# Rests of up to 64 rows of two experts share a page, 72 tiles in place of 79

## What is computed

```python
scores = softmax(xt @ Wg.T)                      # 2048 tokens, 16 experts in 4 groups
gidx   = top_k(max of scores in each group, 2)   # two groups of a token
topi   = top_k(scores in those groups, 4)        # four experts of a token
weights = scores[topi]
h = silu(einsum('td,eid->eti', xt, W1)) * einsum('td,eid->eti', xt, W3)   # 176 wide
expert_out = einsum('eti,edi->etd', h, W2)
y = einsum('etd,te->td', expert_out, combine)    # combine holds the weights
z = silu(xt @ Ws1.T) * (xt @ Ws3.T) @ Ws2.T      # shared experts
x = layernorm(x + y + z)
```

## Time and profile before

| | us |
|---|---|
| median of 3 runs | 1193.8 |
| lowest and highest | 1188.15, 1194.08 |
| the profiled execution | 1193.7 |
| its span, first to last instruction | 1191.9 |
| TensorE busy (matmuls) | 1087.6 (91%) |
| VectorE busy | 496.3 (42%) |
| ScalarE busy | 504.1 (42%) |
| POOL busy | 439.9 (37%) |
| mean granted TensorE clock | 0.964 |

### The profile page before, as it was taken

The page is one execution under the profiler, slowest core; times in us unless marked ns, Lnnn a source line. Parts: engine busy times, 40 slices in busy tenths (PEclk is TensorE's granted clock), DMA queues, the critical chain, the costliest instruction groups (busy, mean ns, idle before and its releaser), DMA issues. The chain is left out here.

```text
span 1191.9 us, 29025 instructions
## 1 busy us (share of the span) xinstructions
PE 1087.6 (91%) x10260; PEld 838.5 (70%) x10261; DVE 496.3 (42%) x1340; ACT 504.1 (42%) x1306; POOL 439.9 (37%) x563
## 2 busy tenths in 40 slices
PE   8889989988898679999988999998789999999998
PEld 4466666655455347777756777786579899899997
DVE  2366665545571113333325666767443800000323
ACT  2444544444432123333334666575344333333333
POOL 2022131311248852777654666332524000200434
PEclk9999999999999669999999999999789999999999
DMA  6199478021283334565536111000157555555673
GB/s 202 45 311 362 161 237 268 21 81 55 118 258 118 129 113 126 154 191 150 144 120 284 37 37 53 22 19 3 56 194 237 187 175 177 174 175 174 194 240 107
DMA packets 119339, 176.09 MB, mean 148 GB/s; under 512 B 17440, under 2 KB 96912, under 8 KB 117776
## 3 DMA queue, kind: packets, MB, share of 16 engines
q1 hardware_dynamic: 94448, 135.55, 34.9%
q0 software_dynamic: 9696, 26.75, 6.9%
q10 hardware_dynamic: 15088, 12.28, 3.1%
HBM read 105.07 MB, written 68.16 MB: 145 GB/s over the span
## 5 line engine op out<-in xcount | busy, mean ns | idle before, releaser
L3149 PE MATMUL bank<-w,m_HT 128*128 x624 | 141.0, 379 | 0.0
L2984 ACT ACTIVATE m_HT<-bank,m_b 128x128 f32<-128x128 f32 x312 | 88.9, 370 | 90.2 <-PE bank L3135 74.2
L3149 PEld LDWEIGHTS bank<-w,m_HT 128*128 128x128 f32 x624 | 115.7, 190 | 14.1
L1820 PE MATMUL bank<-m_W,m_XGT 128*128 x316 | 114.0, 485 | 9.0 <-ACT m_XGT L1677 6.8
L1434 POOL DMA_INDIRECT GA<-ys,r_pos x64 | 64.7, 1010 | 62.9 <-DVE m_US L1764 43.0
L1677 ACT ACTIVATE m_XGT<-bank 128x256 f32<-128x256 f32 x79 | 30.3, 384 | 129.2 <-DVE m_US L1764 80.1
L1756 DVE TENSOR_TENSOR m_H<-bank,m_SG 128x176 f32<-128x176 f32 x79 | 26.9, 341 | 135.7 <-ACT m_SG L1681 96.9
L2948 POOL DMA_INDIRECT m_GA<-ys,r_pos x32 | 31.6, 986 | 133.6 <-SPq L2904 124.9
L3135 PE MATMUL bank<-m_XGT,m_w1a 128*128 128x128 f32 x640 | 77.3, 279 | 2.6 <-issue 1.8
L1820 PEld LDWEIGHTS bank<-m_W,m_XGT 128*128 128x128 f32 x316 | 56.6, 199 | 30.2 <-issue 14.3
L3135 PEld LDWEIGHTS bank<-m_XGT,m_w1a 128*128 128x128 f32 x640 | 75.0, 195 | 3.5 <-issue 2.3
(11 more groups left out here) (475 smaller groups left out, 2301.3 us busy)
## 6 DMA issues: line engine op xcount, KB each, us to landing
m_w1a<-in_m_w SPq DMA_DIRECT2D x20, 1024.0 KB
m_w<-in_m_w SPq DMA_DIRECT2D x19, 1024.0 KB
xs<-zeros SPq DMA_DIRECT2D x1, 10112.0 KB, 34.2
ys<-zeros SPq DMA_DIRECT2D x1, 10112.0 KB, 34.6
ys<-m_US ACTq DMA_DIRECT2D x79, 128.0 KB
m_GS<-xs SPq DMA_DIRECT2D x72, 128.0 KB
w<-in_m_w SPq DMA_DIRECT2D x8, 1024.0 KB, 11.9
xs<-zeros SPq DMA_DIRECT2D x1, 6400.0 KB, 23.7
```

The source lines that it names most:

```text
L1820: last = nc.tensor.matmul(BU[b % 2][:, 0:IW], XGT[:, b % 2, m * P:(m + 1) * P], W13[:, m, bass.ds(e, 1), :], start=m == 0, stop=m == KC - 1)
L2984: last = nc.scalar.activation(HT[:, b % 2, at, :], BU[i][:, c * P:(c + 1) * P], ACT.Gelu, bias=b1[:, b % WB, at:at + 1])
L3149: last = nc.tensor.matmul(BY[b % 2][:, 0:DIM], HT[:, b % 2, c, :], w2[:, bass.ds(e, 1), c, :], start=c == 0, stop=c == CH - 1)
```

## The change

An expert's rest, the rows behind its last full page, no longer takes a page of its own if it has at most 64 rows. Two such rests share a page: one in its lower 64 rows, one in its upper 64. The padding is counted in half pages: `NS0 = ceil(((8192 + 16*63) // 64) / 2) = 72`. Shared pages are the last eight (`MIXED0 = 8`), so tiles 64 to 71 (`PURE = 64`) are computed as if they had two experts, whether they have or not. The table gets a fourth row, `second`, the expert of the upper half.

- Routing: `halves` in place of the last part of `on_dve`, some more steps in `order_on_dve` and `ready_on_dve`.
- TensorE in tiles 64 to 71: each matmul of the up and down product is two, with 64 stationary columns each, into rows 0 to 63 and 64 to 127 of the bank; the second takes its weights from `UPS` and `DOWNS`.
- VectorE copies the second expert's weights there (`keep_up` five steps ahead, `keep_down` three), three sets in turn, in the memory of `Z`.
- Straight code for the last 12 (TensorE), 16 (VectorE) and 8 (ScalarE) tiles; the moments at tile 44, the root after token tile 7, the apply within step 62.
- `EARLY` is 11: token tiles 11 to 15 are gathered in rounds 0 to 4 of `layer1`.

```diff
+HALF = P // 2
+MIXED0 = E0 // 2
...
+    def halves(self, do, dve, v, c, count, slots, total, thresholds, rank_bank):
+        e, k, pad = self.e, self.k, self.e // 2
+        each = lambda ap: ap.unsqueeze(1).broadcast_to([P, TILES, e])
+        nt, single = self.nt[:, 0, pad:], self.nt[:, 1, pad:]
+        do(dve, v.tensor_scalar(self.low[:], count, float(HALF), None, ALU.subtract))
+        do(dve, v.tensor_tensor(c, self.low[:].unsqueeze(2).broadcast_to([P, e, TILES]),
+                                thresholds.unsqueeze(1).broadcast_to([P, e, TILES]), ALU.is_gt))
+        do(dve, v.tensor_reduce(nt, c, AX, ALU.add))
+        do(dve, v.tensor_scalar(self.most[:], nt, float(P), None, ALU.mult))
+        do(dve, v.tensor_tensor(single, count, self.most[:], ALU.is_gt))
+        src, dst, d = self.nt, self.ends, 1
+        while d < e:
+            do(dve, v.tensor_tensor(dst[:, :, pad:], src[:, :, pad:], src[:, :, pad - d:pad + e - d], ALU.add))
+            src, dst, d = dst, (self.ends2 if dst is self.ends else self.ends), 2 * d
+        ends, first, self.singles, self.single = src[:, 0, pad:], dst[:, 0, pad:], src[:, 1, pad:], single
+        self.end_tile, self.first_row = ends, first
+        do(dve, v.tensor_tensor(slots, slots, rank_bank[:, 0:TILES * e].rearrange("p (t e) -> p t e", e=e), ALU.add))
+        do(dve, v.tensor_tensor(first, ends, nt, ALU.subtract))
+        do(dve, v.tensor_scalar(first, first, float(P), 0.0, ALU.mult, ALU.add))
+        do(dve, v.tensor_scalar(self.from_page[:], ends[:, e - 1:e], float(self.slot_tiles - e // 2), None, ALU.max))
+        do(dve, v.tensor_scalar(self.move[:], ends, self.from_page[:, 0:1], -2.0, ALU.subtract, ALU.mult))
+        do(dve, v.tensor_tensor(self.move[:], self.move[:], self.singles, ALU.add))
+        do(dve, v.tensor_tensor(self.move[:], self.move[:], single, ALU.subtract))
+        do(dve, v.tensor_tensor(self.masked[:], slots, each(self.most[:]), ALU.is_ge))
+        do(dve, v.scalar_tensor_tensor(out=self.masked[:], in0=each(self.move[:]), scalar=float(HALF), in1=self.masked[:],
+                                       op0=ALU.mult, op1=ALU.mult))
+        do(dve, v.tensor_tensor(self.slot[:], slots, each(first), ALU.add))
+        do(dve, v.tensor_tensor(self.slot[:], self.slot[:], self.masked[:], ALU.add))
...
-EARLY = 12
+EARLY = 11
...
-                    if t == 9:
+                    if t == 7:
                         fx.l1.root_on_pool(nc, pool, fx.neghalf, own)
...
-                tile_pipeline(act, step, NT)
+                tile_pipeline(act, step, NT, peel=8)
...
+                    if ahead is None:
+                        return
+                    if 0 <= j + 5 - PURE < MIXED0:
+                        keep_up(j + 5 - PURE)
+                    if 0 <= j + 3 - PURE < MIXED0:
+                        keep_down(j + 3 - PURE)
+                    if j == 62:
+                        fx.l1.apply_on_dve(nc, dve, fx.X)
+                def keep_up(n):
+                    e = experts[n] = dve.value_load(r.second[0:1, PURE + n:PURE + n + 1], min_val=0, max_val=E0 - 1)
+                    if n == 0:
+                        dve.wait_ge(z_added, 2 * TILES)
+                    r.steps(dve, nc.vector.tensor_copy(UPS[:, n % SETS].unsqueeze(2), W13[:, :, bass.ds(e, 1), :]))
+                    up_step[n] = r.steps.k
+                def keep_down(n):
+                    e = experts.pop(n)
+                    nc.vector.tensor_copy(DOWNS[:, n % SETS, 0:1, :], W2A[:, bass.ds(e, 1), :])
+                    r.steps(dve, nc.vector.tensor_copy(DOWNS[:, n % SETS, 1:2, :], W2B[:, bass.ds(e, 1), :]))
+                    down_step[n] = r.steps.k
...
-                tile_pipeline(dve, step, NT, ((56, lambda: fx.l1.moments_on_dve(nc, dve, fx.X, r.steps)),
-                                              (68, lambda: fx.l1.apply_on_dve(nc, dve, fx.X))))
+                tile_pipeline(dve, step, NT, ((44, lambda: fx.l1.moments_on_dve(nc, dve, fx.X, r.steps)),), peel=16)
...
+                    if mixed is not None:
+                        pe.wait_ge(r.steps.sem, up_step[mixed])
...
+                        nc.tensor.matmul(BU[b % 2][0:HALF, 0:IW], XGT[:, b % 2, m * P:m * P + HALF],
+                                         W13[:, m, bass.ds(e, 1), :], start=m == 0, stop=m == KC - 1)
+                        last = nc.tensor.matmul(BU[b % 2][HALF:P, 0:IW], XGT[:, b % 2, m * P + HALF:(m + 1) * P],
+                                                UPS[:, mixed % SETS, m, :], start=m == 0, stop=m == KC - 1)
...
+                    pe.wait_ge(r.steps.sem, down_step[k])
+                    for c, w2 in enumerate((W2A, W2B)):
+                        nc.tensor.matmul(BY[b % 2][0:HALF, 0:DIM], HT[:, b % 2, c, 0:HALF], w2[:, bass.ds(e, 1), :],
+                                         start=c == 0, stop=c == 1)
+                        last = nc.tensor.matmul(BY[b % 2][HALF:P, 0:DIM], HT[:, b % 2, c, HALF:P],
+                                                DOWNS[:, k % SETS, c, :], start=c == 0, stop=c == 1)
...
-                tile_pipeline(pe, step, NT)
+                tile_pipeline(pe, step, NT, peel=12)
...
-        fx.NS0 = (TOKENS * TOP0 + E0 * (P - 1)) // P
+        fx.NS0 = -(-((TOKENS * TOP0 + E0 * (HALF - 1)) // HALF) // 2)
```

More of the change, by code:

```diff
@@ L1002, in __init__ @@
         self.gmax, self.grank = sb("gmax", [P, TILES, max(groups, 1)]), sb("grank", [P, TILES, max(groups, 1)])
-        self.nt, self.ends, self.ends2 = (sb(n, [P, e // 2 + e]) for n in ("nt", "ends", "ends2"))
+        rows = [2] if groups else []
+        self.nt, self.ends, self.ends2 = (sb(n, [P, *rows, e // 2 + e]) for n in ("nt", "ends", "ends2"))
+        self.fields = 4 if groups else 3
+        if groups:
+            self.most, self.move, self.own2 = (sb(n, [P, e]) for n in ("most", "move", "own2"))
+            self.from_page, self.at_half = sb("from_page", [P, 1]), sb("at_half", [P, 1])
+            self.upto_half, self.of_half = sb("upto_half", [P, 2, e]), sb("of_half", [P, 2])
         self.hot = sb("hot", [P, k, TILES, e])
@@ L1116, in on_dve @@
         count, slots = self.upto[:, TILES - 1, :], dst[:, pad:]
+        if self.groups:
+            do(dve, v.tensor_tensor(slots, self.upto, total, ALU.subtract))
         if not self.groups:
@@ L1213, in order_on_pe @@
         pe.wait_ge(self.steps.sem, self.table_step)
-        nc.tensor.matmul(table_bank[:, 0:3 * self.slot_tiles], ones[:], self.vals[:].rearrange("p i n -> p (i n)"),
+        nc.tensor.matmul(table_bank[:, 0:self.fields * self.slot_tiles], ones[:], self.vals[:].rearrange("p i n -> p (i n)"),
                          start=True, stop=True).then_inc(self.counted, 1)
@@ L1408, with tile_pipeline @@
 PEEL = 7
-def tile_pipeline(engine, step, n, visits=(), done=0):
-    for at, visit in (*visits, (n - PEEL, None)):
+def tile_pipeline(engine, step, n, visits=(), done=0, peel=PEEL):
+    for at, visit in (*visits, (n - peel, None)):
         with engine.Fori(done // 4, at // 4) as i:
@@ L1419, in tile_pipeline @@
         done = at
-    for j in range(n - PEEL, n):
+    for j in range(n - peel, n):
         step(j, j % 4, n - 1 - j)
```

83 lines of the change are left out of this document (58 added, 25 removed).

## The result

The changed kernel takes 1177.47 us (median, 1173.65 to 1178.36) where the kernel before took 1192.85 (four executions, the three of the table ahead of the prediction among them): 15.4 us less by the medians, 13.2 by the ratio, which is 0.9889 with a 95% interval of 0.9856 to 0.9922 (9.3 to 17.2 us). The record doesn't name the chip of this first comparison. The forecast was 1188.4, with a range of 1181 to 1197. Sign right, size wrong by 10.9 us. In three further groups of runs, on two chips, the ratio was 0.9905 (0.9873 to 0.9938), 0.9938 (0.9916 to 0.9960) and 0.9895 (0.9874 to 0.9917): 11.3, 7.4 and 12.5 us. Both that spread and the median have to be explained.

The account below looks back on a forecast made before the run. The prediction took the first expert stage, in its full stretch, to be bound by TensorE alone. Its terms, -17.5 + 2.9 + 5.3 + 1.5 + 2.5 = -5.3 us, took 1193.7 to 1188.4 us, range 1181 to 1197.

Parts of the forecast that it names:

- Part 1: First expert stage: seven tiles fewer on TensorE, at 2.497 us each, give -17.5 us.
- Part 2: Routing: more vector instructions ahead of the positions, which POOL's first scatter waits for, cost +2.9 us.
- the scatter, the end of it and the start of the full stretch move by as much: POOL's scatter: its start, its end and TensorE's full stretch all come 2.9 us later.
- Part 3: Last eight tiles: halved products run two at a time, +0.66 us each, +5.3 in all; weight copies +1.5.
- rival (a): Shared tiles: the halves run serially, eight tiles cost 19.7 us in place of 5.3, total 1202.8; chance 0.08.
- a change of shape: Shared tiles on TensorE: switching array shape costs some 0.1 us, four times a tile, so 0.4.
- the half-pass tail: Shared tiles on TensorE: half a pass left at the end of each product, 0.15 + 0.11 = 0.26 us.
- Rival (b): Weight copies: VectorE, blocked by POOL, lags and TensorE waits, +8 us in place of 1.5, total 1194.9; chance 0.17.
- Part 4: Moved steps: moments, root and apply cost 0; EARLY 11 adds a gather round in layer 1, +2.5 us.
- 0, for the root is a short POOL instruction: Layernorm: moving the root up two token tiles costs nothing, with only POOL's own next fetch behind it.
- They leave the full stretch, not the scatter's, since the scatter's length is unchanged: First expert stage: the seven tiles leave the steady stretch; eight or so stay in the time of the 64 scatters.
- The forecast's own sign of being wrong: First expert stage: the prediction is wrong if, among other signs, the full stretch doesn't start 2.9 us later.

Follow-up runs that it names:

- before_warm: The kernel before with six more TensorE products of 256 columns in each of the first twelve tile steps: 1204.91 us.
- after_warm: The changed kernel with six more TensorE products of 256 columns in each of the first twelve tile steps: 1196.53 us.
- after: The changed kernel in the first comparison and its trace, against the kernel before: 1177.47 us, ratio 0.9889.
- early12: The changed kernel with EARLY 12 in place of 11: 1193.05 us, ratio 0.9959 to the kernel before.
- tiles72: The kernel before with 72 tiles in place of 79, apply at tile 60, eight tiles peeled, EARLY still 12: 1216.78 us, ratio 1.0154.
- groups 2, 3 and 4: Sets of runs beside the kernel before, each on one chip: group 1 on chip 4, 2 and 4 on chip 13, 3 and 5 on chip 9.
- before: The kernel before, unchanged, in the first comparison and its traces: 1192.85 us in the first comparison.
- delay: The kernel before with ten more vector instructions ahead of the positions, three of 256 columns and seven of 16: 1198.19 us, ratio 1.0011.
- after_third: The changed kernel, unchanged, a third time, beside the kernel before in group 3: 1190.38 us, ratio 0.9938.
- whole_products: The changed kernel with whole products in the last eight tiles and no weight copies, second experts left out: 1189.75 us, ratio 0.9928 to the kernel before.
- after_again: The changed kernel, unchanged, in a second session, group 2: 1178.59 us, ratio 0.9905 to the kernel before.
- after_fourth: The changed kernel, unchanged, once more in group 4: 1177.90 us, ratio 0.9895 to the kernel before.
- halves_in_turn: The changed kernel with all lower-half products written ahead of the upper-half ones in place of alternating: 1177.74 us.
- after_gap: The changed kernel with two more products of 256 columns ahead of the up product in each of the first eight steps: 1182.10 us.
- moved72: The kernel before with 72 whole pages and the change's moved steps, EARLY 11 and peel counts, no halves or copies: 1175.93 us, ratio 0.9895.
- before_fourth: The kernel before, unchanged, in group 5: 1140.48 us.
- delay_again: The kernel before with ten more vector instructions ahead of the positions, again, in group 5: 1142.88 us, ratio 1.0002.
- before_warm8: The kernel before with three more TensorE products of 256 columns in each of the first eight tile steps: 1203.55 us.
- before_third: The kernel before, unchanged, a third trace, beside the changed kernel in group 3: 1196.94 us.

## Why the prediction was wrong

**Part 1, the price of seven tiles: right (where they leave from was not, see below).** 2.50 us a tile in both kernels' full stretch (2.50 to 2.52 from y10 to y59 in all traces but before_warm and after_warm); y10 to y59 takes 122.5 us in after (442.93 to 565.40), and 49 x 2.497 is 122.4.

**Part 2, the way to the positions: right at its start, too dear at its end.** The first scatter is at 344.97 us on the mean of nine traces with the halves, at 341.79 on that of nine without: +3.2 for the forecast 2.9, single traces 2 us to either side. But the last scatter moves by 1.9 between the same two sets (437.55 and 435.68). The step "the scatter, the end of it and the start of the full stretch move by as much" failed by 1.0 us: the 64 scatters of the later start took a little less time.

**Part 3, shared tiles: mechanism right, the size too large by 2.6 us.** The halves run two at a time, rival (a) is out. The period is 3.09 us, +0.59 for the forecast 0.66: the rows' turning, the up product, the product's turning and the down product each take 0.15 us longer (0.37 against 0.22, 1.33 against 1.19, 0.37 against 0.21, 1.01 against 0.87), so a change of shape and the half-pass tail are one cost and not two. That is 0.6 us of the 2.6. The copies cost one wait of 0.42 us, not 1.5, which is 1.1 us of the 2.6. Rival (b) never came, though a wide copy did double beside POOL. The rest, 0.9, is probably that the last tiles drain, 1.2 to 1.5 us apart, where the forecast charged a full 0.66 to each of the eight. The page "TensorEngine Tiling (Array Packing)" of the Trainium skill, section "Key Properties", says both that tiles operate independently and that a switch of the tiling mode drains TensorE. The trace agrees with the first (starts 0.01 us apart); of the second it shows 0.15 us for each switch, and not the drain itself.

**Part 4: right.** The fifth gather round is 28.0 us in place of 25.6, +2.4 for 2.5. early12 shows the other side: with the gather kept in the stage, layer 1 starts 7.2 us late, for 2.4 given back. tiles72 shows what I had costed at nothing: without the earlier root TensorE waits 15.4 us. "0, for the root is a short POOL instruction" holds for the change as made.

With the measured terms the sum is -17.5 + 1.9 + 4.2 + 2.4 = -9.0 us in place of -5.3. Three things agree with it. The group in which both kernels show the same stretch gave -7.4 (-10.1 to -4.8). The other groups' intervals by the ratio hold 9.0 or miss it by under 1 us (9.3 to 17.2, 7.4 to 15.1 and 9.9 to 15.0 us less), so the executions alone barely tell these gains from 9.0; that there is a surplus rests on the traces. And a line fitted through all executions of a group, time against mean granted clock with an offset for the changed kernel, puts that offset at -8.9 (standard error 1.1), -7.7 (0.7) and -9.6 (1.1) in groups 2, 3 and 4. The fit takes the clock as given, which it may not be: among the traces without added products, the stretches with more waiting are those with the lower clock.

**The step that failed** is the one under Part 1: "They leave the full stretch, not the scatter's, since the scatter's length is unchanged". The tiles inside the scatter's stretch were taken as a constant of the kernel ("eight or so"). The forecast's own sign of being wrong came: the full stretch did not start 2.9 us later, y10 came 4.7 earlier. The tiles in the stretch are no constant: from 390 to 436 us the traces show 6 result copies (before, three times, and also delay, tiles72, after_third, early12 and whole_products), 8 (after, after_again, after_fourth, halves_in_turn, after_gap), 9 (moved72), 18 (before_fourth) and 19 (delay_again). Of the 6.4 us between 9.0 and 15.4, two tiles more are 5; the last scatter came 1.1 us later in this pair of traces where 1.9 is the mean. The terms that were too dear (1.0 in part 2, 2.6 in part 3) are the other 3.6 of the miss. A single trace of before could not show that the stretch varies, but it did show that in it no visible work explains the 7 to 10 us between two copies, and I didn't ask what does.

**What is settled and what isn't.** Shown: in the first pair of traces the surplus over 9.0 us lies in that stretch; it can be missing with the change in place (after_third, whole_products), and the short distance can be there without the halves (moved72). The idle time there is of a kind that can vanish for the unchanged kernel (before_fourth). Not shown: that the change brings the two tiles. Outside the first comparison the form goes with the chip: 11.8 to 14.4 us of distance in all seven traces of groups 1 and 3 without added products for TensorE, 3.9 to 6.1 in the four of groups 2 and 4. The unchanged kernel was not traced on chip 13, where only its times are known, 1179 to 1197 us, wide enough to hold both forms. The one pair that differs is the first, from one trace each, and whether the two ran on one chip isn't on record. That a higher clock doesn't bring the tiles is likely from before_warm8, but its added products took time of their own. Open too: why engines wait there for nothing that the profile names. Since groups 3 and 5 bear the same chip number and differ by 56 us, it need not be the chip; what else differed isn't on record. What the change is worth where the kernel before takes 1142 us was not tried: there the fifth round should cost nothing, and a later scatter no longer holds up a TensorE that waits for nothing.

No kernel here that serves every routing beats the changed one; halves_in_turn equals it.

## What to carry to other kernels

When you cost tiles out of a steady stretch, look also at the stretch ahead of it: if its pace is set by idle time that ends in "issue" or "remote", it need not be a constant, and two more traces of the unchanged kernel, at other times and on other chips, are the cheapest experiment there is. Trace both kernels side by side on each, for a form that comes and goes by itself looks like an effect of the change. Shortening one stage counts only once all that other engines owe at its end is moved as well (tiles72 lost 19 us, moved72 gained 12 to 14). Take a second, independent product into the other half of the array's columns whenever a padded tile has half its rows empty: it cost 0.6 us on top of 2.5 here, not another 2.

## What the runs showed of the hardware

- Two half products (128 rows, 64 columns each) with different stationary and moving data start 0.01 us apart and take together what a whole one takes (0.30 us a pass of 352 columns, from 580.06 to 580.36 in after); written one series behind the other they still run in pairs (halves_in_turn).
- Each switch between whole and half products costs 0.15 us, the tail of the half product in it (after, four switches in a period of 3.09 us against 2.50).
- The unchanged kernel took 1190 to 1198 us in four groups and 1142 in a fifth. Most of the difference lies where POOL issues indirect DMAs while other engines hand work to each other: 2.5 us a tile (before_fourth) in place of 8.0 (before), and 25.6 us a round in place of 28.0.
- Three added products a step lifted the granted clock from 395 to 440 us from 0.59 (before_third) to 0.85 (before_warm8, same group); the time was 5 us longer, not shorter.
